# Graph layer on one NeuronCore: gathered groups placed by a table, parts of x read in place as weights, a ring of eight, b2 added last

## What is computed

```python
msg   = x[src] + edge                                  # 53125 x 128
neigh = segment_sum(msg, dst, num_segments=3125)
rst   = (1 + eps) * x + neigh
h     = rst @ W1 + b1                                  # 3125 x 256
h     = relu((h - mean(h, 0)) * rsqrt(var(h, 0) + 1e-5) * gamma + beta)
out   = layernorm(x + h @ W2 + b2)                     # 3125 x 128
```

## Time and profile before

| what | value |
|---|---|
| time, median of 3 runs | 280.74 us (280.03 to 281.6) |
| the profiled execution | 281.48 us, of which 279.7 are its span |
| granted TensorE clock, mean | 0.964 |
| busy share PE / DVE / ACT / POOL | 88% / 75% / 47% / 65% |

### The profile page before, as it was taken

One profiled execution on the slowest core, in us unless ns is written; L12 is line 12 of the kernel. 1 busy time (PEld: TensorE's weight loads), 2 busy tenths in 40 slices (PEclk: granted clock), 3 DMA queues, 4 the chain that ended last, 5 costly groups with the idle time before them and its releaser, 6 DMA issues.

```text
span 279.7 us, 7102 instructions
## 1 busy us (share of the span) xinstructions
PE 244.9 (88%) x2211; PEld 200.6 (72%) x2211; DVE 208.4 (75%) x916; ACT 131.7 (47%) x236; POOL 181.2 (65%) x117
## 2 busy tenths in 40 slices
PE   1567989999998889988899999999999859999970
PEld 1456768899987677766788888777878648844870
DVE  3888997788998778778489887876867861178990
ACT  0327864455555535545255544444443302086494
POOL 2078888888888888888888888888888920000000
PEclk9999999999999999999599999999999968999995
DMA  5955766687888777788488888776665200000033
GB/s 165 285 172 108 147 145 137 156 191 197 189 195 185 178 164 171 181 179 183 96 172 192 174 195 171 167 179 145 150 126 105 53 2 0 2 0 1 2 114 116
DMA packets 49535, 38.39 MB, mean 137 GB/s; under 512 B 5083, under 2 KB 48523, under 8 KB 49497
## 3 DMA queue, kind: packets, MB, share of 16 engines
q1 hardware_dynamic: 32829, 30.62, 38.2%
q0 software_dynamic: 14976, 6.82, 20.4%
q10 hardware_dynamic: 1692, 0.48, 0.9%
HBM read 36.31 MB, written 1.60 MB: 136 GB/s over the span
## 4 chain that ended last, share of the span: by engine, by line
PE 46%; DMA 16%; issue 14%; POOL 9%; DVE 7%; ACT 4%; SPq 2%; DVEq 0%; ACTq 0%; POOLq 0%
PE ps L641 18%; PE ps L649 12%; DMA egat<-in_x_dram,srci 9%; POOL egat L402 9%; DMA egat<-in_edge_attr_dram 7%; PE ps L679 5%; PE ps L673 4%; PE ps L595 4%; ACT big L527 3%; PE ps L665 2%; SPq L321 1%; DVE big L1033 1%; DVE big L1035 1%; PE ps L670 1%; DVE hit_l L904 1%
## 5 line engine op out<-in xcount | busy, mean ns | idle before, releaser
L402 POOL DMA_INDIRECT egat<-in_x_dram,srci x104 | 172.2, 1656 | 44.0 <-issue 29.2
L488 ACT ACTIVATE big<-ps 128x500 f32 x156 | 95.1, 610 | 119.8 <-PE ps L679 91.6
L641 PE MATMUL ps<-big,xp 128*128 128x114 f16 (+8 forms) x675 | 116.9, 280 | 0.2 <-issue 0.2
L649 PEld LDWEIGHTS ps<-hit_c,ebuf 128*128 128x128 f32 x624 | 101.8, 194 | 16.6 <-DVE aggT L983 6.1
L649 PE MATMUL ps<-hit_c,ebuf 128*128 128x20 f32 x624 | 95.1, 230 | 9.1 <-DVE aggT L983 5.0
L641 PEld LDWEIGHTS ps<-big,xp 128*128 128x128 bf16 x675 | 63.0, 110 | 14.6 <-issue 1.1
L983 DVE TENSOR_TENSOR aggT<-aggT,ps 128x20 f32 x208 | 35.8, 172 | 49.8 <-PE ps L649 39.7
L910 DVE TENSOR_TENSOR hit_k<-iota_k,key 128x400 f16<-128x400 f16 x156 | 56.1, 359 | 0.0
L904 DVE TENSOR_TENSOR hit_l<-iota_k,lo 128x256 f16<-128x256 f16 x156 | 52.1, 334 | 1.7 <-issue 1.6
L679 PE MATMUL ps<-hit_k,hit_l 128*128 128x400 f16 x156 | 52.3, 335 | 0.0
L908 DVE TENSOR_TENSOR hit_k<-iota_k,key 128x300 f16<-128x300 f16 x156 | 48.2, 309 | 0.0
(11 more groups left out here) (101 smaller groups left out, 165.5 us busy)
## 6 DMA issues: line engine op xcount, KB each, us to landing
ebuf<-in_edge_attr_dram SPq DMA_DIRECT2D x78, 256.0 KB
egat<-in_edge_attr_dram SPq DMA_DIRECT2D x51, 128.0 KB
egat<-in_x_dram,srci POOLq DMA_INDIRECT x104
out_dram<-big SPq DMA_DIRECT2D x6, 256.0 KB
w_sb<-in_L_gnn_W_dram ACTq DMA_DIRECT2D x2, 128.0 KB, 6.8
rows<-in_dst_dram SPq DMA_DIRECT2D x1, 192.0 KB
rows<-in_src_dram ACTq DMA_DIRECT2D x1, 192.0 KB
egat<-in_edge_attr_dram SPq DMA_DIRECT2D x1, 66.0 KB
```

The lines of the kernel that those rows point to most:

```text
L402: return nc.gpsimd.indirect_dma_start(to, None, x[:, :], bass.IndirectOffsetOnAxis(ap=ix, axis=0), compute_op=op)
L488: nc.scalar.activation(cnt[:, :, bass.ds(lows[m % LOADS], WIN)], ps[:, m % BANKS_C, 0:KEYS].rearrange("p (t n) -> p t n", n=WIN), ACT.Copy ...
L641: last = nc.tensor.matmul(ps[:, ACC + f % 2, 0:SIZES[f]], xp[:, t, n, :], cnt[:, t, STARTS[f]:STARTS[f] + SIZES[f]], start=(u == 0), stop= ...
L649: last = nc.tensor.matmul(ps[:, SUMS + w % BANKS_S, 0:WIN], rows_v[:, j * D:(j + 1) * D], hits_v, start=(j == 0), stop=(j == ROWS - 1))
```

## The change

Four edits:

1. `arrange()` replaces the rule "every fourth". It walks the windows with a clock of its own, in cycles (2400 to a microsecond): a window is gathered when the clock has reached `GATHER_FIRST + n * GATHER` for the n-th gathered group; each window then adds a cost to the clock.
2. `xp` goes. `multiply` takes its first two weights in place, from the upper halves of `xN` and of `xr` (16-bit elements four bytes apart), the third from `x3`. `xr` holds all tiles. ACT's 14 copies go, and the waits of DVE's `rest` for them.
3. `RING_K` is 8; `AHEAD` stays 3.
4. As `xN` is now a weight up to the last unit, POOL's b2 add waits for `block_multiplied` = 9, the end of the last block, in place of the copies.

```diff
-RING_K = 6
+RING_K = 8
+ROUNDS = 12
+SUM = 670
+COUNT = 770
+KEPT = 810
+HITS = 2400
+TURN = 1680
+GAP = 14
+GATHER = 9360
+GATHER_FIRST = 27000
...
-    def in_window(w):
-        return (w + 1) * NG // G > w * NG // G
+    def arrange():
+        order = [(w + 1) * NG // G > w * NG // G for w in range(G)]
+        for _ in range(ROUNDS):
+            ready = spans([w for w in range(G) if not order[w]])
+            now, m, n, order = 0, 0, 0, []
+            for w in range(G):
+                gathered = n < NG - 1 and w < G - 1 and (m == GC or now >= GATHER_FIRST + n * GATHER)
+                gathered = gathered or w == G - 1
+                f, u0, u1 = share(ready, w)
+                own = SUM if gathered else max(SUM + COUNT + KEPT * (m < KEEP), HITS)
+                now += own + (u1 - u0) * (SIZES[f] + GAP) + TURN * (X_RATE * w < NT)
+                order.append(gathered)
+                m, n = m + (not gathered), n + gathered
...
+        return order
...
-        xp = sb("xp", [P, NT, PARTS, D], BF16)
+        xr = sb("xr", [P, NT, D])
+        x3_room = sb("x3_room", [P, NT * D // 2])
...
-                pool.wait_ge(x_first_made, NB)
+                pool.wait_ge(block_multiplied, F)
...
-                        nc.scalar.activation(xp[:, t0:t1, 0, :], upper(xN[:, t0:t1, :]), ACT.Copy).then_inc(x_first_made, 1)
-                        act.wait_ge(x_rest_made, b + 1)
-                        nc.scalar.activation(xp[:, t0:t1, 1, :], upper(xr[:, b % 2, 0:t1 - t0, :]),
-                                             ACT.Copy).then_inc(x_middle_made, 1)
...
-                        last = nc.tensor.matmul(ps[:, ACC + f % 2, 0:SIZES[f]], xp[:, t, n, :],
+                        part_v = x3[:, t, :] if n == 2 else upper((xN, xr)[n][:, t:t + 1, :])[:, 0, :]
+                        last = nc.tensor.matmul(ps[:, ACC + f % 2, 0:SIZES[f]], part_v,
```

More of the change, by code:

```diff
@@ L49 @@
 KEEP = 24
+ROUNDS = 12
[7 more added lines that the diff above has]
+GATHER_FIRST = 27000
+ACT_FROM = 5
 def gnn_layer(nc, x, src, dst, edge, eps, w1, b1, gamma, beta, w2, b2, out):
@@ L82, in gnn_layer, with spans, share @@
     KEYS = NT * WIN
-    def in_window(w):
-        return (w + 1) * NG // G > w * NG // G
-    C_AT = [w for w in range(G) if not in_window(w)]
-    G_AT = [w for w in range(G) if in_window(w)]
+    UNITS = NT * PARTS
+    def spans(c_at):
+        return [c_at[g - 1] + SETTLE for g in ENDS[:-1]] + [G]
+    def share(ready, w):
+        for f in range(F - 1):
+            if ready[f] <= w < ready[f + 1]:
+                n, i = ready[f + 1] - ready[f], w - ready[f]
+                return f, UNITS * i // n, UNITS * (i + 1) // n
+        return 0, 0, 0
+    def arrange():
[11 more added lines that the diff above has]
+                m, n = m + (not gathered), n + gathered
+            short = NG - sum(order)
+            at = [w for w in range(G) if not order[w]]
+            for w in at[len(at) - short:] if short > 0 else []:
+                order[w] = True
+        return order
+    IN_WINDOW = arrange()
+    C_AT = [w for w in range(G) if not IN_WINDOW[w]]
+    G_AT = [w for w in range(G) if IN_WINDOW[w]]
     C_OF = {w: m for m, w in enumerate(C_AT)}
     G_OF = {w: n for n, w in enumerate(G_AT)}
-    READY = [C_AT[g - 1] + SETTLE for g in ENDS[:-1]] + [G]
-    UNITS = NT * PARTS
+    READY = spans(C_AT)
     def units(w):
[L95 to L99, removed]
+        return share(READY, w)
     EARLY = STARTS[-1] // BANK
@@ L151, in gnn_layer @@
         xN = sb("xN", [P, NT, D])
-        xp = sb("xp", [P, NT, PARTS, D], BF16)
+        xr = sb("xr", [P, NT, D])
+        x3_room = sb("x3_room", [P, NT * D // 2])
+        x3 = x3_room[:, :].bitcast(BF16).rearrange("p (t d) -> p t d", d=D)
         aggT = sb("aggT", [P, N + WIN])
@@ L164, in gnn_layer @@
         b2e = sb("b2e", [P, D + 1])
-        rows = sb("rows", [P, 2, QW + 2])
+        rows = x3_room[:, 0:2 * (QW + 2)].rearrange("p (a c) -> p a c", a=2)
         dstq = rows[0:Q, 0, 0:QW + 1].bitcast(I32)
         srcq = rows[0:Q, 1, 0:QW].bitcast(I32)
-        xr = rows[:, :, 0:QW].rearrange("p a (t d) -> p a t d", d=D)
         firsts = sb("firsts", [1, G], I32)
@@ L236, in gnn_layer @@
         x_rest_made = sem("x_rest_made")
-        x_first_made = sem("x_first_made")
-        x_middle_made = sem("x_middle_made")
         x_last_made = sem("x_last_made")
@@ L492, in _ @@
                         scale_x(m)
-                    if m % SPREAD == SPREAD // 2 - 1 and m // SPREAD < NB:
-                        b = m // SPREAD
-                        t0, t1 = pieces(b)
-                        nc.scalar.activation(xp[:, t0:t1, 0, :], upper(xN[:, t0:t1, :]), ACT.Copy).then_inc(x_first_made, 1)
-                        act.wait_ge(x_rest_made, b + 1)
-                        nc.scalar.activation(xp[:, t0:t1, 1, :], upper(xr[:, b % 2, 0:t1 - t0, :]),
-                                             ACT.Copy).then_inc(x_middle_made, 1)
             act.wait_ge(weights_loaded, 80)
@@ L631, in multiply @@
                         if f == 0 and u % (4 * PARTS) == 0:
-                            pe.wait_ge(x_first_made, t // 4 + 1)
-                            pe.wait_ge(x_middle_made, t // 4 + 1)
+                            pe.wait_ge(x_rest_made, t // 4 + 1)
                             pe.wait_ge(x_last_made, t // 4 + 1)
@@ L927, in rest @@
                     t0, t1 = pieces(b)
[L928 to L931, removed]
+                    nc.vector.tensor_tensor(xr[:, t0:t1, :], xN[:, t0:t1, :], upper(xN[:, t0:t1, :]),
                                             ALU.subtract).then_inc(x_rest_made, 1)
@@ L936, in part_3 @@
                     t0, t1 = pieces(b)
-                    v = xr[:, b % 2, 0:t1 - t0, :]
+                    v = xr[:, t0:t1, :]
                     dve.wait_ge(x_rest_made, b + 1)
-                    nc.vector.tensor_tensor(xp[:, t0:t1, 2, :], v, upper(v), ALU.subtract).then_inc(x_last_made, 1)
+                    nc.vector.tensor_tensor(x3[:, t0:t1, :], v, upper(v), ALU.subtract).then_inc(x_last_made, 1)
                 def add_block(f, done):
```

## The result

The changed kernel is slower: 293.32 us (median of 4 runs, 293.04 to 294.23) against 280.38 (279.57 to 281.6), a ratio of 1.046 with a 95% interval of 1.042 to 1.051. The forecast was 295, slower.

The account below looks back on a forecast made before the run. PE bounds most places, POOL about windows 63 to 115 and near 160, one collision at 218. Landing 217.9 plus tail 39.9 puts hidden 14.5 us later: 281.48 + 14.5 = 296.0 profiled, forecast 295, range 286 to 303.

Parts of the forecast that it names:

- POOL's stream is fixed: POOL's gathers: no window order can pull them ahead; the 102nd gather ends at 215.11 us, 3.86 us a group.
- The landing: From POOL's gather end to PE's start on the gathered rows: taken as 2.8 us, so window 184 starts at 217.9.
- The tail: PE's work from window 184 to the start of hidden: 39.9 us, putting hidden at 257.8, 14.5 us later.
- Where the waits begin: PE waits at each gathered group from about window 51 to the 51st group: over 30 waits, some 25 to 35 us.
- The rival of a half clock across window 184: PE's clock halves across window 184 after idling, costing up to 3.3 us: 298 to 299 us; chance 0.08.
- The rival called the other side: PE does not wait for POOL at window 184, the collision's end is a net gain: 278 us; chance 0.04.
- b2 at the end: POOL's add of b2 moves into hidden: collision at 218 goes, 7.55 us add hidden, price nothing; full lock 5.3 us.
- Weights in place: PE's loads of 16-bit weights at a step of four bytes: nothing to 11 us, taken as nothing.
- Ring and copies: Ring of eight gives nothing; dropping ACT's 14 copies (8 us, first windows) gives nothing or a lead lost again.
- The table: Its clock runs too fast, so the 51st gathered group stands at window 184, not 203; PE waits there for POOL.

Follow-up runs that it names:

- half the gathers: Changed kernel, new table kept, with only the first of each gathered group's two gathers issued: 262.45 us, ratio 0.944 to the kernel before.
- the table alone: Kernel before with arrange() and its constants in place of in_window, x packed, ring of six, b2 where it was: 301.28 us, ratio 1.072.
- a ring of six: Changed kernel with RING_K = 6: 293.71 us, ratio 1.043 to the kernel before.
- The mended pair: Changed kernel with the table's clock mended, 264.00 us, beside the kernel before with that table and b2 last (x packed, RING_K = 6), 264.15 us.
- all but the table: Changed kernel with every fourth window gathered as before: 275.06 us, ratio 0.979 to the kernel before.
- b2 last alone: Kernel before with POOL's add of b2 also waiting for the end of the last block: 274.81 us, ratio 0.976.
- the mended table: Changed kernel, counted window costed as the larger of 2400 cycles and PE's products with units: 264.46 us, 0.952; on another chip 264.00, 0.942.

## Why the prediction was right, step by step

**POOL's stream is fixed.** Right as to the window order: the 51st group ended at 215.10, against 215.11, and half the gathers took the waits away altogether. It is fixed to some 1.2 us only (214.4 to 216.8 over eleven profiles).

**The landing.** Taken as 2.8 us, measured as 1.83 (216.93 - 215.10). Too long by 1.0. The groups just ahead of it, at windows 178 and 181, show 1.8 too, and so does window 184 in the table alone and with a ring of six. I had averaged over the waits in the middle, where the DMA engines' share was 0.79; from 207 to 217 it is 0.52 to 0.58 here. That a less busy DMA system lands sooner fits these numbers, but was not tried alone. The trace of the kernel before had the answer in part: its window 159 starts 2.00 us behind the end of its gathers (172.76 to 174.76), without a wait, which 2.8 would not allow.

**The tail.** 39.9 us forecast, 255.93 - 216.93 = 39.00 measured. By its terms: 217.71 - 216.93 = 0.78 for window 184 (forecast 0.9); 248.26 - 217.71 = 30.55 from window 185 to the first load of window 206 (forecast 15.5 + 14.8 + 1.0 = 31.3, so the windows of 1.18 us held and nearly all of the miss is here); 255.93 - 248.26 = 7.67 for the rest (7.7). The two misses, of landing and tail, 1.0 and 0.9, are the whole distance from the forecast 257.8 to 255.93, and from 296.0 to the profiled 294.23.

**Where the waits begin.** Wrong, without weight for the sum. I said window 51, over 30 waits and 25 to 35 us. The first wait for a gather is near 91 us, at window 70, and there are 17 of 18.0 us. The two numbers behind it were both off. I gave PE some 4 us in hand; window 18 came 12.6 us behind the end of its gathers, nearly 10 more than the 2.8 of the landing, since PE came later, not POOL sooner: at window 11 PE waited 1.49 us, the clock then stood at 0.50 from 35.7 to 45.9, and window 33 came at 62.1 instead of 58.0. And I let the lead shrink by up to 1.1 us a group; from window 18 to window 66 it fell from 12.6 to 3.9 in 13 groups, 0.68 each, as PE took 3.2 us a group and not 2.8. And behind 91 the half-clock stretches filled with slow work what would otherwise have been idle time. Since the 51st group's gathers set window 184, none of this changed the end. The rival of a half clock across window 184 did not come: the last slow stretch ended near 196, and from 217 the clock was 1.00.

**The rival called the other side.** Badly priced, without weight for the sum. It gave 278 us to a kernel in which PE does not wait for POOL, with window 184 at 200.9 as before. With half the gathers window 184 came at 184.80 and the time was 262.45: the 200.9 held waits and half clock of its own.

**b2 at the end.** Right in each part. No DVE instruction waited for POOL: the last block's add took 0.27 us as before and the statistics 0.69, with one SBUF input each, beside the add. By the Trainium skill (page "SBUF — State Buffer", section "Who interferes with whom") a VectorE instruction with one SBUF input, outside the two-port modes, does not contend with GpSimd, and the trace agrees. Alone the move is worth 2.4%.

**Weights in place.** Right to take nothing of nothing to 11 us. While PE waits for POOL the changed kernel would hide a slower load, but its last 39 us have no gap, and there the last block's 75 loads (PE and loads alone, clock, DMA) take as long as before:

```profile
239.53:243.27 3.74, 3.71 (x77) 3.73 (x75) 1.00 0.02 4
```

```profile
252.19:255.94 3.75, 3.71 (x77) 3.73 (x75) 1.00 0.02 4
```

The first line is the kernel before, packed; in the second two loads of three are at a step of four bytes. The mended pair agrees, 264.00 and 264.15 us. By the Trainium skill (page "TensorE: Matmul & The Clock Gate", section "Weight-path perf modes — Fast Weight Load (FWL) and DoubleRow") the fast load takes packed or strided columns, and with 109 to 111 ns against 108 and 109 the runs agree.

**Ring and copies.** Right: nothing, by the ring of six and by all but the table.

**The table.** Right in its cause: the error was shown by mending one expression, which turned 4.6% slower into some 5% faster. Of these, b2 last alone gives 2.4; the mended table itself is worth some 3 to 4% (0.952 and 0.942 against 0.979 for all but the table). The constants for PE were sound; the fault was to add the units on top of a bound that belongs to another engine. One reading in the prediction is off: the 0.82 us of window 72 belong to block 2, of 256 columns (blocks counted from 0), and not to block 3. The table priced a counted window of block 2 at 1.24 us where PE takes 0.82, and one of block 3 at 1.28 where PE takes 0.87 with half the gathers, so 3.9 us of the table were over after some 3.67 windows.

## What to carry over

When one engine's stream runs free from the start, its n-th result has a fixed time; the price of an order is the largest, over n, of that time plus the other engine's work behind the n-th use. Moving uses earlier looks harmless where the two paces are close, and is paid in full at the last early use. A planner's cost per step should be the maximum over engines of each one's whole work in the step; check its total against the trace before trusting its placements. The first table planned 251.6 us for the windows, where 227 were measured with waits; the mended one plans 207.2, and 208 were measured.

## What was not expected of the hardware

POOL's add of 128 x 3200 took 6.97 to 6.98 us in the ten profiles where it ran beside `hidden`, and 7.55 and 7.54 in the kernel before and in the table alone, where it caught DVE. The extra 0.57 us do not show that DVE held POOL up: in these two kernels the add's record begins while that of the last gather still runs. In the kernel before:

```profile
217.31 1.54 POOL L402 DMA_INDIRECT egat<-in_x_dram,srci  x1 [0.30 <-issue]
```

This gather ends at 218.85, and the add is put at 218.30, 0.55 us sooner; in the table alone it is 0.57. The DVE instruction that was caught had started ahead of the add, at 218.06, and ended 0.16 us behind it (226.01 against 225.85), where the others of its kind take 0.28. To have begun first did not save it. Why it was not done before the add began is not shown.

The clock fell to half for about 10 us from 35.7, where the kernels with every fourth window gathered kept it at 1.00. Ahead of it, from 22 to 35.7, PE had been busy for 12.04 of 13.7 us, with one gap of 1.49 us; the kernel before was busy for less, 11.60 us of the same stretch. In the table alone it fell at nearly the same place. The mended table has a slow stretch there too, of some 3 us in one profile and 7 in the other. What in the order of the first windows brings this about was not tried.
